# A two-turn loop with a register for V's slot, a new order around the gates, and the last group's rows in pieces

## The reference, cut to what matters

```
x = x + mLSTM(LN(x), ctx, ctx)           # 4 heads, gates i and f from q, k, v; decay matrix
                                         # D = exp(cumulated log f + i - row max), C = (q k^T) * D,
                                         # h = C v / max(|sum C|, exp(-max)), h normalised per head
x = x + LN(x) @ ternary(W0)^T * mean|W0|
x = x + softmax(LN(x) Wq (ctx Wk)^T / 16) (ctx Wv)
x = x + down(silu(gate(xq)) * up(xq))    # xq = LN(x) rounded to 8 bits per row by its maximum,
                                         # weights ternary, the product rounded per row as well
```

## Time and profile before

| What | Value |
|---|---|
| median of 3 runs | 762.22 us (762.09 to 762.45) |
| the profiled execution | 761.56 us, of which the span is 759.8 us |
| PE busy | 683.4 us, 90% of the span |
| DVE, ACT, POOL busy | 622.4, 574.1, 393.1 us |
| one steady turn of phase 1 (369.34 to 399.66) | 30.32 us: PE 28.34, DVE 26.05, ACT 24.95, POOL 15.85 busy |
| FFN, 640 to 700 us | PE busy 59.73 of 60, DVE 55.36, ACT 49.23 |

### The profile page before, as it was taken

One profiled execution on the slowest core, in us unless ns is written; L12 is line 12 of the kernel. 1 busy time (PEld: TensorE's weight loads), 2 busy tenths in 40 slices (PEclk: granted clock), 3 DMA queues, 4 the chain that ended last, 5 costly groups with the idle time before them and its releaser, 6 DMA issues.

```text
span 759.8 us, 16211 instructions
## 1 busy us (share of the span) xinstructions
PE 683.4 (90%) x4942; PEld 520.6 (69%) x4942; DVE 622.4 (82%) x1629; ACT 574.1 (76%) x1298; POOL 393.1 (52%) x618
## 2 busy tenths in 40 slices
PE   5889999999999989899899999975788999999996
PEld 4677786886877867678688687763455566666664
DVE  4786789888898898688988889886488899999994
ACT  3448587887887978679788788775587788888885
POOL 2363463555544734456355564452146566666665
PEclk9969999999999999999999999988799999999999
DMA  9101012122021221212212201012413424244421
GB/s 301 61 1 57 29 56 85 40 73 82 18 84 43 71 85 43 60 41 72 84 36 78 76 24 56 16 43 58 139 35 105 114 79 131 76 131 93 120 76 57
DMA packets 72663, 55.56 MB, mean 73 GB/s; under 512 B 20093, under 2 KB 72318, under 8 KB 72582
## 3 DMA queue, kind: packets, MB, share of 16 engines
q1 hardware_dynamic: 64134, 50.37, 22.2%
q10 hardware_dynamic: 8448, 4.20, 1.9%
HBM read 29.39 MB, written 20.97 MB: 66 GB/s over the span
## 4 chain that ended last, share of the span: by engine, by line
PE 56%; ACT 22%; DVE 13%; issue 6%; POOL 1%; ACTq 1%; DMA 0%; DVEq 0%; POOLq 0%
PE bank L632 10%; PE bank L521 7%; PE bank L597 7%; PE bank L582 7%; ACT nrm L734 7%; PE bank L649 5%; ACT D L782 4%; PE bank L618 4%; ACT raw L700 4%; DVE C L1279 3%; PE bank L641 3%; DVE hmax L1282 2%; PE bank L512 2%; PE bank L590 2%; ACT vg L771 2%
## 5 line engine op out<-in xcount | busy, mean ns | idle before, releaser
L933 POOL TENSOR_TENSOR rs<-ve,minus_half 128x4 f32<-128x4 f32 x64 | 64.7, 1010 | 171.9 <-DVE ve L1060 170.4
L632 PE MATMUL bank<-WGU,fqT 128*128 128x512 bf16 x512 | 126.7, 388 | 10.9 <-ACT D L866 5.0
L1279 DVE SCALAR_TENSOR_TENSOR C<-bank,fback,D 128x1024 f32<-128x1024 f32 x64 | 82.1, 1283 | 15.7 <-ACT D L866 11.2
L632 PEld LDWEIGHTS bank<-WGU,fqT 128*128 128x128 bf16 x512 | 49.0, 99 | 65.4 <-DVE C L1279 15.0
L866 ACT ACTIVATE D<-bank,fback 128x1024 f32<-128x1024 f32 x64 | 71.3, 1114 | 22.6 <-PE bank L632 21.8
L870 ACT ACTIVATE fhT<-bank 128x1024 f16<-128x1024 f16 x64 | 65.5, 1024 | 19.8 <-PE bank L641 19.0
L1282 DVE TENSOR_REDUCE hmax<-C 128x1 f32<-128x1024 f32 x64 | 78.1, 1220 | 2.2
L552 PE MATMUL bank<-WX,qcT 128*128 128x268 f32 x256 | 75.1, 417 | 0.0
L734 ACT ACTIVATE nrm<-x,shift,rs 128x256 f32<-128x256 f32 x128 | 66.9, 617 | 7.6 <-POOL shift L940 7.6
L1006 POOL TENSOR_SCALAR wtmp<-C,hscale 128x1024 f32<-128x1024 f32 x64 | 71.7, 1121 | 0.3 <-issue 0.2
L1054 DVE BATCH_NORM_STATS2 st<-x 128x6 f32<-128x256 f32 x192 | 67.2, 412 | 0.9 <-DVE x L1253 0.3
(11 more groups left out here) (176 smaller groups left out, 1633.5 us busy)
## 6 DMA issues: line engine op xcount, KB each, us to landing
out_dram<-x SPq DMA_DIRECT2D x32, 512.0 KB, 3.2
xg<-in_x_dram SPq DMA_DIRECT2D x16, 512.0 KB, 3.5
cg<-in_ctx_dram SPq DMA_DIRECT2D x16, 512.0 KB, 5.0
rows_q<-fq ACTq DMA_DIRECT2D x16, 256.0 KB, 2.3
xg<-out_dram SPq DMA_DIRECT2D x8, 512.0 KB, 4.6
cg<-out_dram SPq DMA_DIRECT2D x8, 512.0 KB, 4.9
raw<-in_L_ffn_w_gate_dram SPq DMA_DIRECT2D x1, 1024.0 KB, 9.1
x<-in_L_ffn_w_up_dram SPq DMA_DIRECT2D x1, 1024.0 KB, 11.5
```

Source lines behind the costliest of these rows:

```text
L632: mm = pe.matmul(ps[k + half], fqT[:, s, c, :], WGU[:, c, which, half * 512:(half + 1) * 512], start=(c == 0), stop=(c == EC - 1))
L1279: dve.scalar_tensor_tensor(out=fh[:, s % 2, :], in0=up, scalar=fback[:, p, s % FB, 1:2], in1=fsil[:, s % 2, :], op0=ALU.mult, op1=ALU.mult ...
```

## The change

Six edits:

1. `STAGES`: TA now stands ahead of GA.
2. DVE: `hh*hr` moves behind `negmax`, the statistics of x1 move from behind the split (`mT`) to directly behind `x1`.
3. ACT: `normalise(1, ...)` becomes the first thing of a turn; the exponentials of the scores go ahead of the two GA copies.
4. The loop of phase 1 is six passes of two turns. The three tensors `vg[r]` become one tensor of 12 rows, and `r = (z + 2) % 3` is worked out in a register inside the loop.
5. The rows of group 15 are done one batch at a time within the FFN: `fq` of group 14 at i = 1, `normalise` at i = 2 to 5, row maxima at i = 6 to 9, scales at i = 10 and 11, `scale_rows` at i = 48 to 51, `fq` at i = 52 and the store at i = 53.
6. SP's wait `written` is split: group 14's rows and all stores of x behind group 11, group 15's rows behind group 13.

```
-          "GA", "WU", "TA", "WT", "O", "WD")
+          "TA", "GA", "WU", "WT", "O", "WD")
...
-        vg = [sb(f"vg{r}", [P, GB, VG]) for r in range(3)]
+        vg = sb("vg", [P, 3 * GB, VG])
...
+        def vg_row(r, b):
+            return vg[:, bass.ds(r * GB + b, 1), :].rearrange("p o n -> p (o n)")
...
-            with eng.Fori(0, (NG - 4) // 6) as j:
-                for k in range(6):
-                    z = 6 * j + k + 2
-                    turn(Banks(BODY, start, z * ROUNDS), z + 2, z + 1, z, z - 1, z - 2, k % 2, (k + 1) % 3)
+            with eng.Fori(0, NG // 2 - 2) as j:
+                for p in range(2):
+                    z = 2 * j + p + 2
+                    turn(Banks(BODY, start, z * ROUNDS), z + 2, z + 1, z, z - 1, z - 2, p, (z + 2) % 3)
...
             def written():
+                sp.wait_ge(q_out, 16 * (NG - 1) + 16)
+                sp.wait_ge(x_out, 16 * NG)
+
+            def all_written():
                 sp.wait_ge(q_out, 16 * NG + 16)
-                sp.wait_ge(x_out, 16 * NG)
...
-            feed_forward(sp, turn, {NG - 5: written})
+            feed_forward(sp, turn, {NG - 5: written, NG - 3: all_written})
...
+            def last_rows(i):
+
+                if i == 1:
+                    whole_rows(NG - 2)
+                if i == 2:
+                    store_rows(NG - 2)
+                if 2 <= i < 2 + GB:
+                    normalise_rows(NG - 1, (i - 2,))
+                late = i - FB * (NG - 4)
+                if 0 <= late < GB:
+                    scale_rows(NG - 1, (late,))
+                if late == GB:
+                    whole_rows(NG - 1)
+                if late == GB + 1:
+                    store_rows(NG - 1)
...
+                if z is not None:
+                    normalise(1, x1, z, nrm_ready[0])
                 if m is not None:
                     key_copy("TB", keyT[q][:, 1, :])
...
                     act.activation(thr[q][:, :], o[:, 0:16], ACT.Exp).then_inc(done, 1)
                 if z is not None:
-                    normalise(1, x1, z, nrm_ready[0])
                     turned_copies("T1", x1T)
...
+            def last_rows(i):
+
+                if 6 <= i < 6 + GB:
+                    row_max(NG - 1, (i - 6,))
+                if i == 6 + GB:
+                    row_scales(NG - 1)
+                if i == 7 + GB:
+                    row_back(NG - 1)
```

More of the change, by code:

```diff
@@ L617, in turn @@
                             moved("WT", b)
[L618 removed]
+                            shut(pe.matmul(o[:, 0:E], ewT[:, b, :], vg_row((r + 1) % 3, b)[:, 0:E],
                                            start=True, stop=True), "O", b)
@@ L692, in scale_rows, with normalise_rows @@
                                    bias=magic[:, 0:1]).then_inc(f_r, 1)
-            def normalise_rows(y):
-                act.wait_ge(shift_ready[3], y + 1)
-                if not isinstance(y, int) or y > 0:
-                    act.wait_ge(f_r, GB * y)
-                for b in range(GB):
+            def normalise_rows(y, batches=range(GB)):
+                if 0 in batches:
+                    act.wait_ge(shift_ready[3], y + 1)
+                    if not isinstance(y, int) or y > 0:
+                        act.wait_ge(f_r, GB * y)
+                for b in batches:
                     act.activation(fn[:, b, :], x3[:, b, :], ACT.Identity, scale=rs[3][:, b:b + 1],
@@ L834, in turn @@
                     scale_rows(y, (0, 1))
-                if n is not None:
-                    o, done = filled("GA")
-                    act.activation(ncs[:, :], o[:, P:2 * P], ACT.Copy)
-                    act.activation(am[:, :], o[:, 0:P], ACT.Copy).then_inc(done, 1)
                 if z is not None:
@@ L844, in turn @@
                                        accum_out=esum[:, b:b + 1]).then_inc(done, 1)
+                if n is not None:
+                    o, done = filled("GA")
+                    act.activation(ncs[:, :], o[:, P:2 * P], ACT.Copy)
+                    act.activation(am[:, :], o[:, 0:P], ACT.Copy).then_inc(done, 1)
                 if weights:
@@ L1097, in row_steps @@
                 dve.tensor_scalar(fs127[:, :], fainv[:, :], 127.0, None, ALU.mult).then_inc(f_sc, 1)
+            def row_steps(y):
+                row_max(y, range(GB))
+                row_scales(y)
+                row_back(y)
             dve.wait_ge(x_in[0], 16)
@@ L1241, in turn @@
                     dve.tensor_tensor(mT[:, :], ncs[:, :], am_run[:, :], ALU.subtract).then_inc(m_ready, 1)
-                if m is not None:
-                    dve.wait_ge(x1_ready, m + 1)
-                    statistics(1, x1, m)
                 if z is not None:
```

51 lines of the change are left out of this document (26 added, 25 removed).

## The result

The changed kernel takes 756.25 us (median of 4 runs, 754.87 to 757.2); the kernel before, in runs beside it, 762.15 us (761.35 to 762.45). The ratio is 0.9926, with a 95% interval of 0.9909 to 0.9943. So it is faster by 0.7%, 5.9 us where 16.2 were forecast. The time lies in the wide range of 738 to 760 us that the prediction named, but outside the 738 to 753 that it gave to its own forecast, and the gain forecast was 2.7 times the one measured. The profiled execution took 757.0 us, with a span of 754.0 against 759.8.

What follows compares the result with a forecast made beforehand. PE was taken to bound phase 1's turns (30.31 us), PE and DVE about equally the FFN. Gains of 7.0 + 3.8 + 5.4 = 16.2 us from 761.56 give 745.4, as a median 746.0; forecast range 738 to 753, wide range 738 to 760.

Steps and rivals of the forecast that it cites:

- 7.0 us gained: Phase 1, new order: turns of 29.8 us, 0.5 less each over fourteen turns; bounds −4 to +24 us.
- a new PE wait ahead of DX, QK or F0 … near 1.5 us in sum: Sign of being right, phase 1: PE waits there for ACT's exponentials or copies, or DVE's C.
- PE's slower clock behind the hole: FFN, hole at 590.13: counted within the 7.8 us that eleven batches lose in the kernel before.
- the product C (f+29.6): Phase 1: DVE's first product C clears F0's bank, so next F0 starts 29.6 us after this F0's start f.
- T1's copies (f+29.1): Phase 1: ACT's T1 copies start at f+28.8, so F0 could start at f+29.1, f being this F0's start.
- `nlf` takes the place of `hh*hr`, f+16.0: Phase 1, DVE: `nlf` starts 16.0 us after F0's start f instead of f+17.1, ending GA's 1.26 us wait.
- rival (c): Phase 1: the turn doesn't get shorter, 30.3 us, giving 753 us, or 757 with 0.3 lost a turn; chance 0.13.
- 3.8 us gained: Phase 1 loop: one jump of 4.8 us replaced by five held jumps of 0.2 each; range 2.5 to 4.8.
- One or two register instructions a turn and engine, in the 29.8 already: Phase 1 loop: the modulo's register instructions, taken as already within the 29.8 us turn.
- 5.4 us gained: FFN, last group's rows in pieces: 7.8 us lost now, less 2.4 for the pieces; range 3.5 to 6.5.
- At the ends … nothing, 1.2 us either way: Second turn and NEXT: TA fills a GA wait, x1 comes some 1.1 us later; set against each other.
- (b): Phase 1 loop: only DVE or ACT fetches anew, 2.1 us a jump, giving 755.5 us; chance 0.12.

Runs made afterwards that it cites:

- e4_fill: The changed kernel with TC's eight transposes on PE done twice, same result; 750.74 us, ratio 0.9862 to the kernel before.
- e8_ctrl: The changed kernel with T2's eight transposes on PE done twice; 753.89 us, ratio 0.9900 to the kernel before.
- e7_nrm_old: The changed kernel with ACT's `normalise(1)` back behind D's exponentials; 753.55 us, ratio 0.9891 to the kernel before.
- e1_loop: The kernel before with edit 4 alone (two-turn loop, V's slot in a register); 761.38 us, ratio 0.9992 to the kernel before.
- e12_reg6: The kernel before, six-turn loop kept, with a ring of four for V and slot z modulo four in a register; 766.92 us, ratio 1.0074.
- e9_x3_two: The changed kernel's two-turn loop and last rows with the turn order of e5_x3; 748.93 us, ratio 0.9838 to the kernel before, the fastest kernel.
- e5_x3: Kernel before plus edits 5 and 6, TA ahead of GA, score exponentials ahead of GA's copies, DVE's x3 ahead of x1's statistics; 752.38 us.

## Why the prediction was wrong, and where it was right

The forecast had phase 1 at 417.7 us from F0 of turn 0 to F0 of turn 14 (428.50 less 10.8); it took 429.52, 11.8 more. e4_fill splits these at 422.52: 7.0 us belong to the clock's fall, 4.8 to turns that are longer than 29.8 even where the clock stays up. e8_ctrl and e7_nrm_old, also without the fall, put the first part at 5.8 and 4.3.

**Edits 1 to 3, "7.0 us gained" (29.8 a turn): the step that failed.** It is the price put on the new wait.
- *The clock.* I foresaw "a new PE wait ahead of DX, QK or F0 … near 1.5 us in sum", and its size was about right: 1.0 to 1.6 ahead of DX and 0.42 ahead of QK. I put its cost at nothing beyond the time that PE stands, which is hidden by the chain. It also moves PE's idle time from two places (1.26 ahead of GA, 0.44 ahead of T1) to shortly ahead of QK, and there PE's clock fell to its lower level in 8 of 15 turns: 7.0 us in phase 1 (e4_fill). With edits 1 to 3 alone it fell in 9 of 15, and the kernel was slower than before. No rival had that. The FFN's term did count "PE's slower clock behind the hole" (the granted clock from 590.00 to 593.40 us is 0.60 in before), and TA behind the old jump had run at 0.56; the same question asked of each new hole would have found it. What decides between a fall and none at 1.4 to 2.0 us (372.59 fast, 403.09 slow) isn't settled; the runs show only the scale above.
- *The path.* I let the next F0 wait for the product C (f+29.6) and for T1's copies (f+29.1), and missed a third way, though I had named a wait ahead of QK: ACT's copy of TC, QK, T1. It is the one that ended last, 6.36 us from the first `nrm` to F0, and would have given f+29.8 with the `nrm` at f+23.4. In size that is only 0.2 us, but it puts QK on the path, so that a slow QK delays F0 by 1.24 us (345.29 and 375.77).
- *The start of the chain.* "`nlf` takes the place of `hh*hr`, f+16.0": with the order alone it nearly does (f+16.06 to f+16.26). In after, from 192 us on, it is at f+16.2 in the turns behind a slow QK and at f+16.8 in the others, and e4_fill alternates between the two. Of the 0.78 in the turn read, 0.37 are gates that start late, 0.3 of it by the register of edit 4. The other 0.41 are `nlf` 2.58 us behind the gates where `hh` came at 2.17 (390.87 to 393.04 in before): 0.2 is the row of the gates, 0.64 us instead of 0.44, and 0.2 is `nlf` waiting for the end of gneg, for which `hh*hr` had not to wait. `glog` was there 0.3 us before. Why the row of the gates takes 0.19 us in some turns and 0.64 in others stays open.

So even with the clock up the changed kernel's turn is 30.35 us, not shorter than before, which was rival (c) with a chance of 0.13. But it holds the register: against e1_loop, which has the register in the old order (30.6), the order gives 0.25 us a turn.

**Edit 4, "3.8 us gained": the jump right, the register mis-sized.** The body of two turns is held, and a jump costs nothing that shows, less than the 0.2 us I took (in e1_loop the turns with a jump are the shorter ones). "One or two register instructions a turn and engine, in the 29.8 already" was wrong: the address costs PE 0.23 to 0.3 us a turn (e1_loop, e12_reg6), 2.8 us or more over 12 turns, so the edit gives 1.4 us of phase 1 in the old order, and no measurable time. What it costs in the changed kernel's own order, where the chain over DVE and ACT sets the turn, I did not measure; the 0.3 us by which the gates come later point to as much, and in the order of e9_x3_two it costs 0.25 (30.2 a turn, where e5_x3 had 29.95). The rule of the Trainium skill that spoke against the edit ("Runtime: NRT & Kernel Launch", section "Instruction fetch mechanics") did not come true on PE for a body of two turns: no jump stalls in after. For DVE and ACT the prediction drew too much from it: the section puts 256 instructions into 16 KiB, so their bodies of 223 and 177 fit into the two pages. With four turns PE and DVE did stall (3.11 and 3.37 us of "issue").

**Edits 5 and 6, "5.4 us gained" (3.5 to 6.5): right.** They give 6.3 us alone (5.0 to 8.1). In the changed kernel products 0 to 14 of the FFN take 43.4 us instead of 51.2. The two holes of the earlier trace rows are gone, a row maximum in pieces costs DVE 0.40 us of its own (0.35 forecast), and PE has no wait on SP's turned rows at i = 60.

**"At the ends … nothing, 1.2 us either way"**: 0.9 us lost between turns 14 and 15; T1 of the last turn waits 4.1 us for its `nrm` where it waited 2.9. In the fastest kernel this step is 3.8 us longer than before (27.35), the next thing to mend there.

**The sum.** Phase 1 was to gain 10.8 us and lost 1.0. The FFN was to gain 5.4 and gained 7.8, of which the stretches around it took 1.4 back and the start added 0.5: 5.9 in all. That the time lies within 738 to 760 is luck: the range reached so far for rivals (b) and (c), not for a fall of the clock.

## What to carry to other kernels

When an order removes a wait of TensorE, look where its idle time goes: the same microseconds in one gap ahead of dense work can cost its clock, here 1.2 us of F0's start each time, since the slow stage stood on the path; moving the consumer that clears the bank (here DVE's x3) ahead of work that is not urgent took the gap away, and cheap work put into it helped as well. When an instruction is moved to the front of a queue, its inputs' own times become the bound: trace each of them back, and don't give it the start time of the one whose place it takes. A loop index that selects a matmul's operand costs TensorE issue time in every turn (0.23 to 0.3 us here), so weigh it against the jumps it saves, and see whether the modulo folds.

## What the runs showed of the hardware that I had not expected

- With up to 1.35 us of idle time ahead of DX and QK, TensorE ran QK in 2.06 to 2.14 us in all of 41 turns; with 1.37 to 2.06 us it ran it in 3.1 to 3.7 us in 15 of 29, at a granted clock of 0.53 to 0.61 where that was read; with 2.2 us or more in all 19. Doubling eight transposes to sixteen made the kernel 5.5 us faster.
- Instructions are held over a jump for a body of two turns (308 on PE, 223 on DVE in the program's count), not for one of four; the jump then costs 4.8 to 5.0 us, as that of six turns does: some 3 us of stall, and 1.4 to 1.6 us because TA behind it runs at a granted clock near 0.55.
- With an operand's address in a register, the first of O's eight matmuls starts 0.26 to 0.30 us late, and the turn is 0.23 us longer.
